# Cross attention: the scores as three float32r products of high and low parts, split by GpSimd

## The reference

```python
x = x + xattn0(layernorm(x), ctx); x = x + attn0(layernorm(x)); x = x + experts0(layernorm(x))
x = x + xattn1(layernorm(x), ctx); x = x + mamba1(layernorm(x)); x = x + ffn1(layernorm(x))
```

```python
qh = (q @ Wq + bq).reshape(B, LQ, HEADS, D_K).transpose(0, 2, 1, 3)
kh = (k @ Wk + bk).reshape(B, LKV, HEADS, D_K).transpose(0, 2, 1, 3)
vh = (v @ Wv + bv).reshape(B, LKV, HEADS, D_K).transpose(0, 2, 1, 3)
scores = jnp.einsum('bhqd,bhkd->bhqk', qh, kh) * scale
attn = jax.nn.softmax(scores, axis=-1)
out = jnp.einsum('bhqk,bhkd->bhqd', attn, vh)
```

## Time and profile before

| what | value |
|---|---|
| time, median of 3 runs | 4387.01 us (4385.79 to 4387.67) |
| time of the profiled execution | 4388.23 us |
| its span | 4386.4 us |
| first cross attention, about | 80 to 1070 us of the span |
| second cross attention, about | 1960 to 3040 us of the span |
| instructions | 133964 |

### The profile page before, as it was taken

One profiled execution on the slowest core, in us unless ns is written; L12 is line 12 of the kernel. 1 busy time (PEld: TensorE's weight loads), 2 busy tenths in 40 slices (PEclk: granted clock), 3 DMA queues, 4 the chain that ended last, 5 costly groups with the idle time before them and its releaser, 6 DMA issues. The chain is left out here.

```text
span 4386.4 us, 133964 instructions
## 1 busy us (share of the span) xinstructions
PE 3791.6 (86%) x54334; PEld 2594.8 (59%) x54335; DVE 2897.2 (66%) x4857; ACT 1979.2 (45%) x2986; POOL 1418.0 (32%) x1573
## 2 busy tenths in 40 slices
PE   6999999999797299939999999998877777777778
PEld 4777777777686266627777777776322222222247
DVE  5666666666466122246666666665899999999974
ACT  2555555555433022106555555555444444444432
POOL 3333333333000200052333333331076666667610
PEclk8999999999898599969999999999899999999989
DMA  1010001000002400020000100000011111111100
GB/s 62 25 33 26 26 26 33 26 26 18 9 0 69 185 31 29 30 79 19 32 26 26 33 26 26 26 26 24 12 35 34 32 33 33 32 36 37 32 26 19
DMA packets 61351, 148.44 MB, mean 34 GB/s; under 512 B 8706, under 2 KB 29218, under 8 KB 60482
## 3 DMA queue, kind: packets, MB, share of 16 engines
q1 hardware_dynamic: 57794, 132.75, 9.3%
q0 software_dynamic: 3072, 8.39, 0.6%
HBM read 123.81 MB, written 17.30 MB: 32 GB/s over the span
## 5 line engine op out<-in xcount | busy, mean ns | idle before, releaser
L692 DVE TENSOR_REDUCE x_maxes<-x_misc_ps 128x1 f32<-128x512 f32 (+1 forms) x1792 | 1045.5, 629 | 574.9 <-PE x_misc_ps L476 574.7
L630 ACT ACTIVATE x_probs<-x_score_ps 128x1024 f32<-128x1024 f32 (+1 forms) x896 | 859.5, 961 | 798.7 <-PE x_score_ps L550 792.4
L1762 POOL TENSOR_TENSOR b_drive<-b_b_all,b_dtx 128x512 f32<-128x512 f32 x512 | 653.8, 1278 | 524.9 <-DVE b_dtx L1833 300.6
L1680 PE MATMUL b_acc_ps<-b_read,ident 128*128 128x512 f32 x1024 | 586.4, 660 | 229.8 <-DVE b_read L1804 229.7
L654 POOL CAST x_kT_hi<-x_kT 128x512 fp32r<-128x512 f32 (+1 forms) x448 | 257.7, 575 | 1459.5 <-PE x_misc_ps L494 978.9
L1786 DVE TENSOR_TENSOR_SCAN b_state<-b_decay_ps,b_drive 128x512 f32<-128x512 f32 x512 | 617.0, 1206 | 0.0
L1745 ACT ACTIVATE b_decay_ps<-b_dt,b_a_neg 128x504 f32<-128x504 f32 x512 | 349.8, 684 | 538.5 <-DVE b_state L1786 538.5
L1680 PEld LDWEIGHTS b_acc_ps<-b_read,ident 128*128 128x128 f32 x1024 | 157.4, 193 | 604.8 <-DVE b_read L1804 603.4
L544 PE MATMUL x_score_ps<-x_qz,x_kT 32*128 32x128 f32 x13312 | 496.3, 283 | 10.1 <-ACT x_probs L630 6.2
L526 PE MATMUL x_misc_ps<-x_probs,x_v 128*32 128x64 f32 x26624 | 464.5, 221 | 0.5 <-issue 0.5
L526 PEld LDWEIGHTS x_misc_ps<-x_probs,x_v 128*32 128x32 f32 x26624 | 392.2, 110 | 103.7 <-issue 87.5
(11 more groups left out here) (280 smaller groups left out, 5442.7 us busy)
## 6 DMA issues: line engine op xcount, KB each, us to landing
x_raw<-in_ctxT SPq DMA_DIRECT2D x64, 800.5 KB, 4.4
b_b_all<-b_b_rows SPq DMA_DIRECT2D x128, 256.0 KB, 3.3
m_w<-in_m_w SPq DMA_DIRECT2D x16, 704.0 KB, 19.2
m_w<-in_m_w SPq DMA_DIRECT2D x8, 768.0 KB, 19.8
m_slot_rows<-m_zero SPq DMA_DIRECT2D x1, 4992.0 KB, 17.4
m_block_rows<-m_slot_rows SPq DMA_DIRECT2D x39, 128.0 KB, 2.0
m_slot_out<-m_out SPq DMA_DIRECT2D x39, 128.0 KB, 1.7
x<-in_x SPq DMA_DIRECT2D x1, 2048.0 KB, 8.1
```

The costliest lines, as they stand in the source:

```text
L630: nc.scalar.activation(probs[rows, s % 2, js, 0:n], score_ps[rows, js, 0:n], ACT.Exp).then_inc(exp_done, 1)
L692: nc.vector.tensor_reduce(maxes[:, c:c + m, j, k0 // NB], bank(op)[:, 0:m * even].rearrange("p (c k) -> p c k", c=m)[:, :, 0:kn], AX.X, AL ...
L1680: nc.tensor.matmul(acc_ps[:, c, :], ident[:, :], read[:, c, :], start=False, stop=True, skip_group_check=True).then_inc(acc_done, 1)
L1762: nc.gpsimd.tensor_tensor(drive[:, c, :], b_all[:, j, :], dtx[:, c, :], ALU.mult).then_inc(drive_done, 1)
```

## The change

The scores (L544) are made of three float32r products in place of one float32 product: high keys with high queries, high keys with low queries, low keys with high queries. `kT_hi` and `kT_lo` now hold a whole batch (two of them, by turns) and `qz_hi` and `qz_lo` three batches. The maxima read the same `kT_hi`. ScalarE copies a projected share into a small float32 buffer `kT` (two shares, by turns), and GpSimd makes the high part by a cast and the low part by a subtraction for each share (`split_keys` in place of `round_keys`). For the queries it makes the masked float32 product, its cast, and the subtraction, in step 3. In its part before the loop, one batch's queries are split before the fill of `v_sb`, and the next batch's behind the first batch's keys.

```diff
@@ tensor: largest
-                    ins = nc.tensor.matmul(dst[:, m * kn:(m + 1) * kn], qz_hi[rows, b % 2, c, :, :].rearrange("p s q -> p (s q)"),
-                                           kT_hi[rows, (b * NG + n) % 2, m * kn:(m + 1) * kn], start=True, stop=True)
+                    ins = nc.tensor.matmul(dst[:, m * kn:(m + 1) * kn], qz_hi[rows, b % 3, c, :, :].rearrange("p s q -> p (s q)"),
+                                           kT_hi[rows, b % 2, c, k0:k0 + kn], start=True, stop=True)
@@ tensor: scores
                 if g == 0:
-                    pe.wait_ge(qz_done, u + 1)
+                    pe.wait_ge(qz_lo_done, u + 1)
+                    pe.wait_ge(kT_lo_done, u * NG + NG)
...
                 for n, (h, c) in enumerate(parts):
-                    for j in range(QUADS):
-                        rows = slice(j * 32, (j + 1) * 32)
-                        nc.tensor.matmul(score_ps[0:kn, j, n * P:(n + 1) * P], kT[rows, u % 2, c, cols(mine[h])],
-                                         qz[rows, u % 2, c, :, :].rearrange("p s q -> p (s q)"),
-                                         start=n == 0, stop=False, skip_group_check=True)
+                    for m, (k, q) in enumerate(((kT_hi, qz_hi), (kT_hi, qz_lo), (kT_lo, qz_hi))):
+                        for j in range(QUADS):
+                            rows = slice(j * 32, (j + 1) * 32)
+                            nc.tensor.matmul(score_ps[0:kn, j, n * P:(n + 1) * P], k[rows, u % 2, c, cols(mine[h])],
+                                             q[rows, u % 3, c, :, :].rearrange("p s q -> p (s q)"),
+                                             start=n == 0 and m == 0, stop=False, skip_group_check=True)
@@ scalar: keep_keys
-                nc.scalar.activation(kT[:, b % 2, c:c + m, k0:k0 + kn],
-                                     bank(op)[:, 0:m * even].rearrange("p (c k) -> p c k", c=m)[:, :, 0:kn], ACT.Copy
-                                     ).then_inc(act_free, 1)
+                if at > 1:
+                    act.wait_ge(kT_lo_done, at - 1)
...
+                nc.scalar.activation(kT[:, at % 2, 0:m * even], bank(op)[:, 0:m * even], ACT.Copy).then_inc(act_free, 1)
@@ gpsimd: queries
+                ).then_inc(qz_done, 1)
+                pool.wait_ge(qz_done, b + 1)
+                if b > 2:
+                    pool.wait_ge(exp_done, 2 * (b - 2) * NG)
+                nc.gpsimd.tensor_copy(qz_hi[:, b % 3, :, :, :], qz[:, :, :, :]).then_inc(qz_hi_done, 1)
+                pool.wait_ge(qz_hi_done, b + 1)
+                nc.gpsimd.tensor_tensor(qz_lo[:, b % 3, :, :, :], qz[:, :, :, :], qz_hi[:, b % 3, :, :, :].bitcast(F32),
+                                        ALU.subtract).then_inc(qz_lo_done, 1)
@@ gpsimd: round_keys becomes split_keys
-                if at > 1:
-                    made(pool, ("M", (at - 2) // NG, (at - 2) % NG, QUADS - 1))
                 read_out(pool, ("K", b, n))
...
-                nc.gpsimd.tensor_copy(kT_hi[:, at % 2, 0:m * even].rearrange("p (c k) -> p c k", c=m)[:, :, 0:kn],
-                                      kT[:, b % 2, c:c + m, k0:k0 + kn]).then_inc(kT_hi_done, 1)
+                full = kT[:, at % 2, 0:m * even].rearrange("p (c k) -> p c k", c=m)[:, :, 0:kn]
+                of = (slice(0, P), b % 2, slice(c, c + m), slice(k0, k0 + kn))
+                nc.gpsimd.tensor_copy(kT_hi[of], full).then_inc(kT_hi_done, 1)
+                pool.wait_ge(kT_hi_done, at + 1)
+                nc.gpsimd.tensor_tensor(kT_lo[of], full, kT_hi[of].bitcast(F32), ALU.subtract).then_inc(kT_lo_done, 1)
@@ gpsimd: the steps
                 if key_share(u, g)[0] < B:
-                    round_keys(*key_share(u, g))
+                    split_keys(*key_share(u, g))
                 if g == 0 and 1 < u + 1 < B:
                     split_context(pool, u + 1, 2)
-                if g == 2 and 1 < u + 1 < B:
-                    pool.wait_ge(exp_done, 2 * u * NG)
-                    queries(u + 1, qz, qz_done)
                 if g == 3 and u + 2 < B:
-                    made(pool, ("M", u, NG - 1, QUADS - 1))
-                    queries(u + 2, qz_hi, qz_hi_done)
+                    queries(u + 2)
                 if g == 5 and u + 2 < B:
                     made(pool, ("V", u * NG + NG - 1))
                     split_context(pool, u + 2, 0)
```

More of the change, by code:

```diff
@@ L388, in cross_attention @@
             project_queries(nc, inner, tag, x_sb, ident, qT, wq, bq, loads, split_first)
[L389 to L392, removed]
+        qz = sb(f"{tag}_qz", [P, KD, 2, LQ])
+        qz_hi = sb(f"{tag}_qz_hi", [P, 3, KD, 2, LQ], F32R)
+        qz_lo = sb(f"{tag}_qz_lo", [P, 3, KD, 2, LQ], F32R)
+        kT = sb(f"{tag}_kT", [P, 2, NB])
+        kT_hi = sb(f"{tag}_kT_hi", [P, 2, KD, LKV + LKV % 2], F32R)
+        kT_lo = sb(f"{tag}_kT_lo", [P, 2, KD, LKV], F32R)
         v_sb = sb(f"{tag}_v", [P, NG, 2, H, 2 * DH])
@@ L409, in cross_attention @@
         qz_hi_done = sem(f"{tag}_qz_hi_done")
+        qz_lo_done = sem(f"{tag}_qz_lo_done")
         kT_hi_done = sem(f"{tag}_kT_hi_done")
+        kT_lo_done = sem(f"{tag}_kT_lo_done")
         misc_ready = sem(f"{tag}_misc_ready")
@@ L599, in keep_keys @@
                 _, b, n = op
+                at = b * NG + n
                 made(act, op)
-                c, k0, kn = SHARES[n][0]
+                if at > 1:
+                    act.wait_ge(kT_lo_done, at - 1)
                 m = len(SHARES[n])
-                even = kn + kn % 2
-                nc.scalar.activation(kT[:, b % 2, c:c + m, k0:k0 + kn],
-                                     bank(op)[:, 0:m * even].rearrange("p (c k) -> p c k", c=m)[:, :, 0:kn], ACT.Copy
-                                     ).then_inc(act_free, 1)
+                even = SHARES[n][0][2] + SHARES[n][0][2] % 2
+                nc.scalar.activation(kT[:, at % 2, 0:m * even], bank(op)[:, 0:m * even], ACT.Copy).then_inc(act_free, 1)
             def keep_values(op):
@@ L637, in _, with queries, split_keys @@
         def _(pool):
-            def queries(b, to, done):
+            def queries(b):
                 nc.gpsimd.tensor_tensor(
-                    to[:, b % 2, :, :, :].rearrange("p c s q -> p c s q"),
+                    qz[:, :, :, :].rearrange("p c s q -> p c s q"),
                     qT[:, :, b * LQ:(b + 1) * LQ].rearrange("p c (s q) -> p c s q", s=1).broadcast_to([P, KD, 2, LQ]),
                     mask[:, :].rearrange("p (c s q) -> p c s q", c=1, q=1).broadcast_to([P, KD, 2, LQ]), ALU.mult
-                ).then_inc(done, 1)
-            def round_keys(b, n):
+                ).then_inc(qz_done, 1)
[6 more added lines that the diff above has]
+                                        ALU.subtract).then_inc(qz_lo_done, 1)
+            def split_keys(b, n):
                 at = b * NG + n
-                if at > 1:
-                    made(pool, ("M", (at - 2) // NG, (at - 2) % NG, QUADS - 1))
                 read_out(pool, ("K", b, n))
@@ L653, in round_keys @@
                 even = kn + kn % 2
-                nc.gpsimd.tensor_copy(kT_hi[:, at % 2, 0:m * even].rearrange("p (c k) -> p c k", c=m)[:, :, 0:kn],
-                                      kT[:, b % 2, c:c + m, k0:k0 + kn]).then_inc(kT_hi_done, 1)
+                full = kT[:, at % 2, 0:m * even].rearrange("p (c k) -> p c k", c=m)[:, :, 0:kn]
[3 more added lines that the diff above has]
+                nc.gpsimd.tensor_tensor(kT_lo[of], full, kT_hi[of].bitcast(F32), ALU.subtract).then_inc(kT_lo_done, 1)
             pool.wait_ge(w_in, 16 * NW)
-            for b in range(2):
-                queries(b, qz_hi, qz_hi_done)
+            nc.gpsimd.memset(kT_hi[:, :, :, LKV:].bitcast(F32), 0.0)
+            queries(0)
             nc.gpsimd.memset(v_sb[:, :, :, :, :], 1.0).then_inc(filled, 1)
             for n in range(NG):
[L662 to L665, removed]
+                split_keys(0, n)
+            queries(1)
+            split_keys(1, 0)
             for s in range(STEPS):
```

## The result

The changed kernel takes 4703.29 us (median of 4 runs, 4698.9 to 4718.4) where the kernel before takes 4387.34: the ratio is 1.0726, with an interval of 1.0701 to 1.0752. It is 316 us slower. The forecast was 248 us slower, 4635 us, with 4690 us as the upper end of the range; the time lies 13 us above it. The profiled execution has 4698.9 us and a span of 4697.1 us.

A forecast was written before the change was run, and what follows sets the result against it. TensorE was taken as the bound. Scores +170.5 and -2.6, GpSimd waits +42 and +50, VectorE's wait -13, initial query split +1.5: +248 us on 4387.01, giving 4635 us; own range 4600 to 4670, 4535 to 4690 with two rivals.

The forecast's parts named there:

- TensorE sets the length of a step, and what is added there is added to the time: Cross attentions: TensorE busy 951.2 of 965 us and 1043.4 of 1060 us, so its added instructions lengthen the time.
- A round costs a load, 0.111 us: +170.5 us: Scores of a full step: twelve rounds at 0.111 us, 1.33 us in place of 0.89 us, 384 times.
- The second rival: Score rounds faster than a load, about 0.081 us, with full GpSimd waits: 4551 us; chance 0.04.
- the third: Rival for the score rounds (L544): only streaming passes charged, 0.056 us a round, -84 us, to 4303 us; chance 0.03.
- the fourth: Rival for the scores: few-column float32r products charged as four times the columns, 0.22 us a round, about 5097 us; chance 0.05.
- the narrow step: Scores with 65-column loads: a round falls to about 0.057 us, 0.34 us for 0.38 us, 64 times, -2.6 us.
- Two new waits on GpSimd: 0.70 us and 0.83 us, 42 and 50 us: Key subtraction delays context splits queued in steps 6 and 0; TensorE waits for each 60 times.
- The first rival: The added GpSimd work is hidden and its waits don't appear: 4543 us; chance 0.12.
- VectorE's wait goes: -13 us: TensorE's 0.21 us a batch waiting for VectorE's maxima goes, as VectorE gets 0.44 us more a step; 62 times.
- TensorE's clock still 1.00: Expected in the profile after: granted clock stays at the 2.4 GHz level; no term in the sum.
- The fifth rival: GpSimd's casts and subtractions each 0.2 us slower through memory sharing, 60 us more: 4695 us; chance 0.06.
- The overlap that the forecast counted: At both GpSimd waits, longer scores bring TensorE 0.44 us later, taken off the 1.27 us delay.

The follow-up runs named there:

- the context first: GpSimd splits the context third before the key share in steps 0, 5 and 6: 4536.91 us in the changed kernel, 4366.43 us in the kernel before.

## Why the prediction was wrong

Point by point, by its own steps:

- **TensorE sets the length of a step, and what is added there is added to the time.** Right but for step 2 (below). Steps 3, 4 and 5 grew by 0.42 to 0.46 us for a forecast of 0.444 us.
- **A round costs a load, 0.111 us: +170.5 us.** Right in its price, 0.111 us in the trace, though step 2 hides its share of the 170.5 us. The second rival (0.081 us a round) and the third (0.056 us) fall by the same rows, and the fourth by the narrow step, where 128 columns stream in a round of 0.060 us. The 81 ns for load and matmul pairs at 128 columns of the Trainium skill, "TensorE: Matmul & The Clock Gate", section "Back-to-back issue gap", are not what these rows show. The narrow step gave 0.05 us for a forecast of 0.04.
- **Two new waits on GpSimd: 0.70 us and 0.83 us, 42 and 50 us.** Right: alone, the first is 0.71 us (0.62 and 0.81); the second is 1.14 us against no wait, of which the kernel before had 0.25 us, so 0.89 us are new. The first rival falls.
- **VectorE's wait goes: -13 us.** Undersized. Step 2 grew by 0.02 and 0.04 us in place of 0.44. The wait for VectorE in that step took up nearly all of the longer scores. The term was 0.41 us a batch, -26 us.
- **"TensorE's clock still 1.00".** This is the step that failed. It was a sentence of the last part and not a term of the sum. It was put at nothing, with no reason given, though the change added two waits to an engine that had been busy without a break. The clock was 0.95 in the attentions: 48 low stretches, some 83 us. Without them the change would have been about 4620 us, 15 us under the forecast and mostly by VectorE's term; with them it is 4703 us, above the range. The fifth rival, which has the nearest time, is wrong in its mechanism: the subtraction took 1183 ns.

What makes the clock fall is shown by kernels with and without the waits (low stretches in the attentions, and their us in all):

| scores | no waits | wait in step 0 | wait in step 1 | both waits | both, filled |
|---|---|---|---|---|---|
| float32 | 0, 0 | | | 11, 48 | |
| three products | 8, 34 | 17, 92 | 33, 160 | 48, 208 | 8, 34 |
| two products | 1, 3 | | | 73, 365 | |

A row across says that TensorE's standing still does it: more waiting, more low stretches, and no more than without waits when the same time is filled with products. A column down says that the scores make it worse: under nearly the same waits, two one-pass products lose the clock 73 times and the full float32 one 11 times. (The three products of the change, 48 times, waited less: from load to load it is 1.14 and 1.34 us in step 0.) That it is the thinner streaming of a one-pass product is the likely reading, but it is not shown: what is shown is the kind of product.

The two halves of the change, taken one by one, are 170 us for the scores (4537 against 4366 us, both with the context first) and 155 us for the subtraction alone. The overlap that the forecast counted is 2 x 0.44 us in 60 batches, 53 us. That leaves 273 us, and 316 us were measured. The difference of 43 us is what the clock costs beyond the 8 and 11 stretches that each half has alone; those have 82 us of low clock, some 33 us by 0.40 for each. It fits the 83 us above.

What stays open is why in the change odd batches lose the clock in step 0 and even ones do not, and what the few low stretches in steps 5 and 6 come from, which are there without any added wait.

## What to carry to other kernels

Before a full float32 product is split into one-pass products, count the weight loads and not the passes: with 128 columns streaming through 128 columns of weights, two one-pass products cost as much as the full one, and the third is a loss. When work is added to an engine whose queue another one reads just in time, put it behind what is waited for: the same 448 subtractions cost 6 us there and 155 us ahead of it. And when a change puts waits into an engine that was fully busy, read the granted clock as a term of its own, above all if the same change makes its products stream less: here two new waits of 0.7 and 0.9 us in a batch, 95 us in all, cost nearly as much again in clock.

## What the runs showed of the hardware

TensorE's clock fell to the 1.2 GHz level behind waits of 0.7 to 1.2 us, in a stage in which it was otherwise busy without a break, and about 0.40 us were lost for each us of it. Under the same order of GpSimd it fell 11 times where a step's eight rounds of scores were full float32 products, and 73 times where they were one-pass products of the same 128 columns.
